# Two softmax-maximum matmuls at a time, twice in each key step, with the score matmuls between the pairs

## The reference, cut to what matters

```python
# attention of layer 0, "att0" below
qk = jnp.einsum('bhqd,bhkd->bhqk', q, k) / jnp.float32(np.sqrt(s))
p = jax.nn.softmax(qk, axis=-1)
p = p * jnp.triu(jnp.ones((s, s)), k=0)
z = jnp.einsum('bhqk,bhkd->bhqd', p, v)
# attention of layer 0's second block and of layer 1, "att1" and "att2"
scores = jnp.where(causal, jnp.einsum('bqhd,bkhd->bhqk', q, k) * scale, lowest)
attn = jnp.einsum('bhqk,bkhd->bqhd', jax.nn.softmax(scores, axis=-1), v)
```

## Time and profile before

| | |
|---|---|
| median of 3 runs | 3010.7 us (3010.32 to 3012.12) |
| the profiled execution | 3020.09 us, of which its span 3018.4 us |
| PE busy | 2528.1 us (84%) |
| DVE busy | 1990.5 us (66%) |
| ACT busy | 1432.9 us (47%) |
| mean granted clock of PE | 0.875 |

### The profile page before, as it was taken

How to read it: one execution, slowest core, us unless ns; L and a number is a source line. 1 busy time by engine, 2 the same in 40 slices (tenths; PEclk the granted TensorE clock), 3 DMA queues, 4 the chain that set the end, 5 groups by cost and what they waited for, 6 DMA issues and landing times. The chain is left out here.

```text
span 3018.4 us, 40035 instructions
## 1 busy us (share of the span) xinstructions
PE 2528.1 (84%) x14544; PEld 1137.5 (38%) x14544; DVE 1990.5 (66%) x4005; ACT 1432.9 (47%) x2105; POOL 391.9 (13%) x562
## 2 busy tenths in 40 slices
PE   4599999999954499899669939998995989799897
PEld 2243333333321233333234414333332446443663
DVE  3788888988715688678345548867963545455453
ACT  1067676777741147547612213673682236432562
POOL 1100001000001100100100020011011323123230
PEclk7599999999986589879879966997997879898898
DMA  5000000000001100000000020000001113110320
GB/s 215 25 23 11 21 10 17 15 10 7 3 18 70 47 24 24 32 11 11 22 1 0 0 80 30 8 28 33 7 8 39 35 61 123 39 35 25 123 96 14
DMA packets 72971, 105.84 MB, mean 35 GB/s; under 512 B 23656, under 2 KB 45800, under 8 KB 71144
## 3 DMA queue, kind: packets, MB, share of 16 engines
q1 hardware_dynamic: 69640, 92.05, 9.0%
q10 hardware_dynamic: 3168, 11.64, 1.0%
HBM read 51.17 MB, written 17.17 MB: 23 GB/s over the span
## 5 line engine op out<-in xcount | busy, mean ns | idle before, releaser
L697 ACT ACTIVATE att_probs<-psum 128x1024 f32<-128x1024 f32 (+3 forms) x1152 | 1037.0, 951 | 717.9 <-PE psum L746 716.2
L655 DVE TENSOR_REDUCE att_part_max<-psum 128x1 f32<-128x512 f32 x1792 | 1128.2, 684 | 177.5 <-PE psum L728 173.8
L728 PE MATMUL psum<-att_k_rows,att_q_rows 64*128 64x512 f32 (+3 forms) x2304 | 842.0, 493 | 150.9 <-DMA att_k_rows<-att_ones 102.5
L728 PEld LDWEIGHTS psum<-att_k_rows,att_q_rows 64*128 64x128 f32 x2304 | 370.4, 200 | 812.3 <-DVE att_part_max L655 526.0
L746 PE MATMUL psum<-att_q_rows,att_k_rows 64*128 64x512 f32 (+3 forms) x2304 | 446.3, 413 | 30.5 <-DMA att_q_rows<-att_max_rows 15.1
L771 PE MATMUL psum<-att_probs,v_aug 128*9 128x512 f32 (+3 forms) x3712 | 450.1, 559 | 14.8 <-ACT att_z_sb L689 14.5
L652 DVE CUSTOM_DVE_ANT_0 att_masked<-psum,mask_max_sb 128x384 bf16<-128x384 f32 (+3 forms) x512 | 234.5, 486 | 116.5 <-PE psum L728 111.1
L746 PEld LDWEIGHTS psum<-att_q_rows,att_k_rows 64*128 64x128 f32 x2304 | 249.0, 196 | 121.1 <-ACT att_probs L697 83.4
L601 POOL TENSOR_SCALAR_AFFINE_SELECT att_probs<-att_probs 128x256 f32<-128x256 f32 x256 | 103.0, 408 | 880.4 <-ACT att_probs L697 878.2
L1352 ACT ACTIVATE latt_probs<-psum,latt_bias,latt_scale 128x192 f32<-128x192 f32 x256 | 127.5, 507 | 123.6 <-DVE latt_bias L1391 123.6
L767 PE MATMUL psum<-att_probs,att_one_only 128*9 128x512 f32 (+3 forms) x1280 | 147.6, 533 | 10.6 <-ACT att_z_sb L689 10.4
(11 more groups left out here) (258 smaller groups left out, 2608.3 us busy)
## 6 DMA issues: line engine op xcount, KB each, us to landing
att_k_rows<-k_pieces SPq DMA_DIRECT2D x48, 256.0 KB
latt_k<-local_k_T SPq DMA_DIRECT2D x32, 384.0 KB, 3.0
att_q_rows<-q_pieces SPq DMA_DIRECT2D x168, 64.0 KB
lproj_table<-in_tables SPq DMA_DIRECT2D x16, 512.0 KB, 3.6
latt_q<-local_q_T SPq DMA_DIRECT2D x32, 256.0 KB, 2.4
latt_v_own<-local_v_tok SPq DMA_DIRECT2D x32, 256.0 KB, 2.3
k_pieces<-proj_piece SPq DMA_DIRECT2D x12, 512.0 KB, 2.8
q_pieces<-proj_piece SPq DMA_DIRECT2D x12, 512.0 KB, 2.7
```

The costliest lines, as they stand in the source:

```text
L655: nc.vector.tensor_reduce(column, ring[e % NRING][:, 0:w], AX.X, ALU.max).then_inc(ring_free, 1)
L697: nc.scalar.activation(probs[s % NPROBS][:, pr, :, at:BANK], st[pr][:, :, at:BANK], ACT.Exp, scale=scale).then_inc(st_free, 1)
L728: nc.tensor.matmul(ring[e % NRING][:, 0:w], q_rows[u % NQ][rows, pr, qt * P:(qt + 1) * P].bitcast(F32R), k_rows[g % 2][rows, pr, kc * BANK ...
```

## The change

It has three parts. `maxima` now waits, ahead of the first tile of a pair, until both banks that the pair will use are free; the second tile then has nothing left to wait for. `issued_by` never ends a half step between the two tiles of a pair: it rounds up by one. And the step's order becomes maxima, scores, maxima, products in place of scores, maxima, products, maxima.

```diff
     def issued_by(self, u, share):
         at = [min(len(self.stream), t + 1 + SPARE) for t in self.turn_at] + [len(self.stream)]
-        return at[u] + round((at[u + 1] - at[u]) * share)
+        count = at[u] + round((at[u + 1] - at[u]) * share)
+        return count + 1 if self.pair_begins(count - 1) else count
+
+    def pair_begins(self, e):
+        return 0 <= e < len(self.stream) and len(self.stream[e]) > 1 and self.stream[e][-1] == 0
...
-                        if e >= NRING:
-                            pe.wait_ge(ring_free, e - NRING + 1)
+                        last = e + 1 if plan.pair_begins(e) else e
+                        if last >= NRING:
+                            pe.wait_ge(ring_free, last - NRING + 1)
...
                 if kb == 0:
                     pe.wait_ge(m_in[u % NQ], MIN_ * (u // NQ + 1))
+                maxima(plan.issued_by(u, (kb + 0.5) / plan.blocks[u]))
                 scores(s, 0)
                 scores(s, 1)
-                maxima(plan.issued_by(u, (kb + 0.5) / plan.blocks[u]))
+                maxima(plan.issued_by(u, (kb + 1) / plan.blocks[u]))
                 if s >= 2:
                     products(s - 2)
-                maxima(plan.issued_by(u, (kb + 1) / plan.blocks[u]))
```

## The result

The changed kernel takes 3097.48 us (median of 4 runs, 3093.1 to 3109.71) against 3011.41 us for the kernel before (its three runs and a fourth beside the changed kernel); the ratio is 1.0291, with a 95% interval of 1.0261 to 1.0321. The forecast was slower, 3063 us; the measured time lies 34 us above it and 7 above the range. The profiled execution of the changed kernel took 3098.5 us.

The account below looks back on a forecast made before the run. It took a closed 2.69 us chain through PE and DVE, neither full, to bound the step. att0's +21.2 and the causal +30.8 gave +52.0 us on the 3010.7 median: 3063 us, range 3032 to 3090.

Parts of the forecast that it names:

- the ordinary step: In the middle of a stage, the step between two groups of products stays at 2.69 us with pairs: 0 change.
- the order alone: In the middle of a stage, the reorder is the same cycle and costs and gives nothing.
- The prologue of att0: Before att0's steps, each pair takes 1.57 us, losing 0.37: +14.4 us, plus 3.7 up to the first products.
- the ninth step: In att0's units, rounding makes this step hold 4 + 2 items: 3.97 us for 3.28, +0.69.
- the end of the stage: At att0's end, the last maxima tile is reduced at +1.0 us against 2.8 before: -2.0 us.
- the turn's step: In att0's units, the turn stands alone in its half step: 2.2 us for 2.55, -0.35.
- att0's sum: Over all of att0: 14.4+3.7+4.6+0.5-2.0 = +21.2 us.
- the units (2, 0): In the causal attentions, a 6.83 us wait for copied maxima covers the cost: 0; without that cover 2 x 3 us.
- some 17 of 32: In causal units (0, 1) and (2, 1), steps at the low clock cost +0.37 us, the others +0.08: +7.5 us.
- the rival: In the causal units, longer PE waits prolong the lower clock: 20 x 1.7 = +34 us, 3097 us; chance 12%.
- (0, 3) and (2, 3): In the causal attentions, these units are like att0's: 4 x 0.33 = +1.3 us.
- the causal prologues: Before the steps of att1 and att2, 16 pairs each at 0.50 clock: +4.5 us, twice, +9.0 us.

Follow-up runs that it names:

- order-only kernel: The kernel before with only the new step order (maxima, scores, maxima, products), keeping old waits and counts; ratio 1.0005.
- the wait alone: The kernel before with only the wait for both banks of a pair, keeping old order and counts; ratio 1.0681.
- the kernel with single prologues: The full change, but each tile in the three prologues waits for its own bank only; 3076.5 us, ratio 1.0198 to the kernel before.
- nearly equal gaps: The kernel before, att0 only: maxima, one head pair's scores, half the products, then the same again; first-step products whole; 2991.66 us, ratio 0.9898.
- the same cut of the products and unequal gaps: The kernel before with value products cut into two 256-column halves, each behind one group of maxima; 3105.6 us, ratio 1.0299.
- the filled one: The full change with two more pairs of unread matmuls behind each pair in the three prologues; 3082.9 us, ratio 1.0212 to the kernel before.

## Why the prediction was wrong

**Right.** That the ordinary step is a chain of 0.54, 0.74, 0.43 and 0.98 us, closed through PE and DVE: it stayed at 2.69 with pairs, at 2.69 with the new order, grew to 3.28 when a tile had to wait for one reduction more (by 0.6, as the expectation had it), and fell to 2.50 once work was put into its waits. That the order alone is nothing: 1.0005. The prologue of att0 (a pair each 1.57 us), the ninth step (3.97), the end of the stage; the turn's step is 2.09 rather than 2.2, its sign right. att0's sum was +21.2 and is +21.2; agreement to a tenth is luck, agreement of the terms is not. That the units (2, 0) hide their cost behind the copied maxima: 26.9 us in the order-only kernel, 26.5 and 26.3 in the full change. (Against the 28.6 and 28.1 of the kernel before they even look shorter, but that is the new order, which starts a unit's first scores, and with them the unit as measured here, behind its first maxima.)

**Wrong: the clock.** The step that failed is the one that let the causal steps keep the clock they had, and counted "some 17 of 32" steps as low, the same before and after. It stood among the rivals, with 12% and 3097 us; that is where the time is, but by a different sum. Low time grew by 82 us, which at 0.22 is 18 us (22 at 0.27). In the rival I had a low six-item step at 5.7 against 3.97, 1.7 us a step or 0.3 per us at the lower level, and 20 steps: +34. The extent was too high (20 steps of 5.7 us, 114 for 82) and the price above the 0.22 to 0.27 measured; the time agreed by luck, because other terms were too low. Against the rival the prediction had said that the order of work in a step is the same; it is, and the low time grew all the same, most where the waits grew most (401 us with the wait alone). That the clock costs this time is shown from two sides: 4.0 us between two passes of one program at 1.00 and 0.79, and a kernel that gets faster by doing 640 matmuls more.

**Wrong: the causal terms themselves.** Of the causal steps' +52.4 the clock is 18 to 22; the remaining 30 to 34 stand against a forecast of 21.8. The parts, from one execution each and with the clock at 0.22: rounding 13, and the pair wait 22. The latter is the full change less rounding and order, 30.5 in the steps (962.1 less 931.6), less 8 for 38 us more of low time. Among the units, (0, 3) and (2, 3) cost about 1.5 at clock 1.00 for a forecast of 0.33, as I took them to be like att0's. Some 0.8 of this is there in the order-only kernel (42.2 us for 41.4), so the order is not free unit by unit; why the rest is larger than in att0 is not shown. Unit (1, 0), for which I put nothing, grew from 9.0 to 11.2 at 1.00 (in the kernel with single prologues) and to 14.0 and 14.4 in the full change, with the clock low in most of it. Of the 2.2 at full clock, 1.7 is the new order: the order-only kernel has 10.7 there, and gives it back in (2, 0), the unit behind. So 0.5 is left for the pairs and some 3 for the clock.

**Wrong: the causal prologues.** +7.4 each for 4.5. The pair wait is 4.7 of it (23.6 less the 18.9 of single waits), as forecast; the other 2.7 is the new order, which puts four tiles ahead of the first scores (2.3 in the order-only kernel). The prediction counted these tiles in att0, but not in the causal attentions, where it had the order cost nothing. In the order-only kernel the prologues are 2.3 longer each and the steps together 1.6 shorter, so at most a third came back.

Of the whole miss of 36 us (88.4 against 52.0 by the table), 18 is the clock, 12 the causal steps and 6 the prologues; at a price of 0.27 it is 22, 8 and 6.

## What to carry to other kernels

When two engines pass a small ring of buffers back and forth, write down the closed chain (issue to consumer, consumer to freed buffer, the in-order work between) before any count of busy time. Grouping issues in twos on a ring of three makes each group wait a full way back, here 1.28 us at clock 1.00 and 1.57 at 0.50, in place of two reductions (1.20); no kernel here gained by it. Here the step got shorter with nearly equal gaps and scores and products in each (2.50 for 2.69 us), and not with the same cut of the products and unequal gaps (2.71). And where the granted clock of a stage is already below 1.00, cost a slower chain a second time: in this kernel the low time grew with the chain, from 202 us to 284, and to 401 with the wait alone.

## What the hardware showed that I had not expected

- The profile's PE busy share does not tell what the clock will do: 99% busy at 0.50 in the old prologue with 82 matmuls in 47.8 us, 77% busy at 0.95 in the filled one with 247 in 54.0. In the old one each record lasts 0.79 us and one begins every 0.60.
- Extra matmuls that fall into waits can be free or better: 640 of them made the full change some 16 us faster in its causal stages and left the kernel before where it was (0.9985).
- Half a group of products costs 0.55 us where the whole costs 0.98: 0.06 us more than half, beside the 0.43 from a maxima load to the products.
